# First-layer experts of a two-layer mixture-of-experts block: the gate and up product made from high and low halves

## What is computed

```python
w, idx = jax.lax.top_k(probs, TOP_K)                       # 8 of 64
gu_e = jnp.einsum('ech,ehf->ecf', buf, expert_gate_up_w)   # [rows of e, 512] x [512, 2 * 256]
act = _silu(gu_e[..., :I]) * gu_e[..., I:]
out_e = jnp.einsum('eci,eih->ech', act, expert_down_w)     # [rows of e, 256] x [256, 512]
y = out_e[e_flat, slot] * w_flat[:, None]                  # summed over a token's 8 experts
```

## Time and profile before

| what | value |
|---|---|
| median of 3 runs | 2224.71 us |
| the profiled execution: time / span | 2228.88 us / 2227.1 us |
| TensorE busy | 2103.2 us, 94% |
| VectorE / ScalarE / GpSimd busy | 59% / 47% / 23% |
| mean granted TensorE clock | 0.976 |
| first-layer experts, first to last tile's start | 695.55 to 1112.48 us |

### The profile page before, as it was taken

How to read it: one execution, slowest core, us unless ns; L and a number is a source line. 1 busy time by engine, 2 the same in 40 slices (tenths; PEclk the granted TensorE clock), 3 DMA queues, 4 the chain that set the end, 5 groups by cost and what they waited for, 6 DMA issues and landing times. The chain is left out here.

```text
span 2227.1 us, 39923 instructions
## 1 busy us (share of the span) xinstructions
PE 2103.2 (94%) x13454; PEld 1518.7 (68%) x13455; DVE 1310.5 (59%) x2799; ACT 1049.0 (47%) x2427; POOL 522.1 (23%) x503
## 2 busy tenths in 40 slices
PE   6999999998998999999978999999989989999998
PEld 3777777775964444444465777788759867777775
DVE  4677777776773222222255777777664437777776
ACT  2466666666321111111133666666665316666655
POOL 4000000001553545445512000000002302223332
PEclk9999999997999999999989999999979999999999
DMA  5001000103142989998831000000032156656661
GB/s 175 29 33 34 22 18 33 34 2 138 38 189 80 332 281 318 321 328 279 257 92 54 22 11 25 28 28 28 1 124 88 39 210 234 253 205 223 228 220 19
DMA packets 63471, 282.47 MB, mean 127 GB/s; under 512 B 13155, under 2 KB 13325, under 8 KB 44005
## 3 DMA queue, kind: packets, MB, share of 16 engines
q1 hardware_dynamic: 43604, 246.88, 30.0%
q0 software_dynamic: 19728, 33.75, 6.9%
HBM read 259.82 MB, written 32.41 MB: 131 GB/s over the span
## 5 line engine op out<-in xcount | busy, mean ns | idle before, releaser
L818 ACT ACTIVATE probs<-ps,less_max 100x360 f32<-100x360 f32 (+1 forms) x384 | 212.0, 561 | 167.5 <-DVE less_max L648 88.3
L1811 PE MATMUL pgu<-ring,xT 128*128 x560 | 267.0, 600 | 6.5 <-issue 3.3
L804 ACT ACTIVATE pTs<-pt 128x300 f32<-128x300 f32 x512 | 189.3, 425 | 128.7 <-PE pt L527 127.6
L1811 PEld LDWEIGHTS pgu<-ring,xT 128*128 128x128 f32 x560 | 99.6, 191 | 114.8 <-issue 114.4
L527 PE MATMUL pt<-ident,probs 100*128 100x100 f32 (+1 forms) x1152 | 137.2, 256 | 30.8 <-ACT pTs L804 27.3
L527 PEld LDWEIGHTS pt<-ident,probs 100*128 100x128 f32 (+1 forms) x1152 | 115.9, 141 | 61.4 <-issue 36.8
L404 PE MATMUL po<-first 128*128 128x512 f32 (+1 forms) x564 | 146.9, 411 | 1.4 <-DVEq L706 1.4
L1899 DVE COPY hT<-ph 128x256 f32<-128x256 f32 x70 | 29.7, 425 | 195.9 <-PE ph L1817 195.9
L404 PE MATMUL pp<-first 128*128 128x512 f32 x564 | 143.2, 402 | 1.2 <-DVE first L428 1.2
L648 DVE CUSTOM_DVE_ANT_0 ps<-ps,madd 100x362 f32<-100x362 f32 (+1 forms) x256 | 128.8, 566 | 23.7 <-PE ps L513 23.5
L400 PE MATMUL po<-first 128*128 128x362 f32 (+1 forms) x720 | 136.9, 339 | 2.8 <-DVE first L437 1.4
(11 more groups left out here) (352 smaller groups left out, 4457.3 us busy)
## 6 DMA issues: line engine op xcount, KB each, us to landing
ring<-in_l_ew SPq DMA_DIRECT2D x64, 1536.0 KB, 9.5
w<-in_l_ew SPq DMA_DIRECT2D x40, 1024.0 KB, 7.9
after<-in_l_ew SPq DMA_DIRECT2D x24, 1024.0 KB, 8.1
xnT<-in_ctxT SPq DMA_DIRECT2D x14, 1444.0 KB, 6.6
first<-in_l_up SPq DMA_DIRECT2D x2, 4096.0 KB, 13.4
b<-in_l_eb SPq DMA_DIRECT2D x8, 1024.0 KB, 4.7
wd<-in_l_down SPq DMA_DIRECT2D x2, 2048.0 KB, 8.7
xn_rows<-mid SPq DMA_DIRECT2D x16, 200.0 KB
```

Source lines behind the costliest of these rows:

```text
L804: act.activation(pTs[:, g % 2, j, 3 * half:3 * half + 3, :].rearrange("k c q -> k (c q)"), pt[:, half, 0:3 * S], ACT.Copy).then_inc(t_out, 1)
L818: act.activation(probs[g % 2 * HPC + j][:, k0:k1], ps[j][0:S, 0:k1 - k0], ACT.Exp, bias=less_max[:, g, seg, j:j + 1], scale=-1.0 if masked ...
L1811: last = pe.matmul(pgu[p][:, :], xT[p][:, c, :], wgu[c], start=c == 0, stop=c == DC - 1)
```

## The change

- `gate_up` in the first layer makes three float32r products a chunk, of high and low halves of rows and of weights, in place of one float32 product: 12 matmuls a tile for four.
- ScalarE gains for each tile a copy of the turned rows (`xT_high`) and a copy of the weights of the tile after the next, 128 x 2048, to `ws_high`. Its order is silu, rows, weights, `y`.
- VectorE's copy of the rows becomes a subtraction out of PSUM (`xT_low`), and it gains a subtraction of the next tile's weights, 128 x 2048 with both inputs in SBUF (`ws_low`), placed between `hT` and `xT_low`.
- TensorE no longer reads the expert's number nor the place for `gate_up`. ScalarE and VectorE read the place. GpSimd reads the expert's number of the tile three ahead, after that tile's gather, waits for `w_ready` there and passes it on as `weights_there`.
- SyncE passes on `w_ready` for three places ahead of the one it replaces, not two. Two small loads for the next stage wait for `parts_done`, as they share memory with the halves.
- The two tables get two more entries, which repeat the last tile.

The diff, with three hunks left out (the first table's two entries, the small loads' wait, the sizes of the tables):

```diff
@@ -1567,6 +1569,7 @@
                         link(dve.scalar_tensor_tensor(out=texp[:, :], in0=turn_of[:, :], scalar=-float(RING),
                                                       in1=texp[:, :], op0=ALU.mult, op1=ALU.add))
                         link(dve.tensor_copy(env.tile_buffer[:, 0:NT], texp[:, :]))
+                        link(dve.tensor_copy(env.tile_buffer[:, NT:NT + 2], texp[:, NT - 1:NT].broadcast_to([1, 2])))
 
                     step = 2 if swiglu else 1
                     evens = tile_n[:, :].rearrange("a (n s) -> a n s", s=step)[:, :, 0]
...
@@ -1657,11 +1660,15 @@
         index_now = [sb(f"index_now{p}", [P, 1], U32) for p in range(2)]
         sum_at = [sb(f"sum_at{p}", [P, 1], U32) for p in range(2)]
         xg = [sb(f"xg{p}", [P, D]) for p in range(2)]
-        xT = [sb(f"xT{p}", [P, DC, P]) for p in range(2)]
+        xT = [sb(f"xT{part}", [P, DC, P], F32R) for part in ("_high", "_low")]
         sg = [sb(f"sg{p}", [P, I0]) for p in range(2)]
         h = [sb(f"h{p}", [P, I0]) for p in range(2)]
         hT = [sb(f"hT{p}", [P, FI, P]) for p in range(2)]
         y = [sb(f"y{p}", [P, D]) for p in range(2)]
+
+        ws = [[sb(f"ws{p}{part}", [P, DC, 2 * I0], F32R) for part in ("_high", "_low")] for p in range(2)]
+        weights_there = sem("weights_there")
+        x_high, gu_high, gu_low, parts_done = sem("x_high"), sem("gu_high"), sem("gu_low"), sem("parts_done")
         px, ph = pb("px", [P, DC, P]), pb("ph", [P, 4, P])
         pgu = [pb(f"pgu{p}", [P, 2 * I0]) for p in range(2)]
         pd = [pb(f"pd{p}", [P, D]) for p in range(2)]
...
@@ -1682,6 +1689,11 @@
         def pairs_of(engine):
             return engine.value_load(env.tile_count[0:1, 0:1], min_val=MIN_PAIRS0, max_val=TILES0 // 2)
 
+        def gate_up_weights(engine, t):
+            at = slice(t, t + 1) if isinstance(t, int) else bass.ds(t, 1)
+            place = engine.value_load(env.tile_buffer[0:1, at], min_val=0, max_val=RING - 1)
+            return ring[:, bass.ds(place, 1), 0:DC, :].rearrange("p a c n -> p (a c) n")
+
         with nc.Block() as block:
             @block.sync
             def _(sp):
...
@@ -1695,14 +1707,14 @@
 
                 def replace(turn, n):
 
-                    ahead = n + 2
+                    ahead = n + 3
                     arrived(ahead % RING, turn - 1 + ahead // RING)
                     e = turn * RING + (n - RING)
                     at = slice(e, e + 1) if isinstance(e, int) else bass.ds(e, 1)
                     ended = sp.value_load(env.tile_ends[0:1, at], min_val=1, max_val=TILES0)
                     sp.wait_ge(d_mm, ended)
                     load(turn * RING + n, n)
-                for n in range(2):
+                for n in range(3):
                     arrived(n, 0)
                 turns, rest = E0 // RING, E0 % RING
                 with sp.Fori(1, turns) as turn:
...
@@ -1761,18 +1775,30 @@
                         out=env.moe_sum[p][:, :], in_=y[p][:, :], in_offset=None, compute_op=ALU.add,
                         out_offset=bass.IndirectOffsetOnAxis(ap=sum_at[p][:, 0:1], axis=0),
                         bounds_check=T - 1, oob_is_err=False).then_inc(added[p], 16)
+                def tiles_weights(t):
+
+                    at = slice(t, t + 1) if isinstance(t, int) else bass.ds(t, 1)
+                    e = pool.value_load(env.tile_expert[0:1, at], min_val=0, max_val=E0 - 1)
+                    pool.wait_ge(w_ready, e + 1)
+                    pool.sem_inc(weights_there, 1)
+                for p in range(2):
+                    tiles_weights(p)
                 for p in range(2):
                     fetch(2 + p, p)
+                for p in range(2):
+                    tiles_weights(2 + p)
                 pool.wait_ge(env.sum_begun, 16 * G)
                 pool.sem_inc(passed, 1)
                 pool.wait_ge(env.x_out, 16 * B)
                 pool.sem_inc(passed, 1)
                 for p in range(2):
                     fetch_next(2, p)
+                    tiles_weights(4 + p)
                     add_rows(0, p, True)
                 with pool.Fori(3, n_pairs + 1) as i:
                     for p in range(2):
                         fetch_next(i, p)
+                        tiles_weights(i * 2 + p)
                         add_rows(i - 2, p)
                 last = last_pair_of(pool)
                 for p in range(2):
...
@@ -1793,22 +1819,21 @@
                         last = pe.transpose(px[:, c, :], rows[p][:, c * P:(c + 1) * P], ident[:, :])
                     last.then_inc(x_mm, 1)
 
-                def weights(t, row):
+                def down_weights(t):
                     at = slice(t, t + 1) if isinstance(t, int) else bass.ds(t, 1)
                     place = pe.value_load(env.tile_buffer[0:1, at], min_val=0, max_val=RING - 1)
-                    return [ring[:, bass.ds(place, 1), row + n, :].rearrange("p a n -> p (a n)")
-                            for n in range(DC if row == 0 else FI)]
+                    return [ring[:, bass.ds(place, 1), DC + n, :].rearrange("p a n -> p (a n)") for n in range(FI)]
 
                 def gate_up(t, p, between):
-                    at = slice(t, t + 1) if isinstance(t, int) else bass.ds(t, 1)
-                    e = pe.value_load(env.tile_expert[0:1, at], min_val=0, max_val=E0 - 1)
-                    wgu = weights(t, 0)
-                    pe.wait_ge(w_ready, e + 1)
+                    pe.wait_ge(gu_low, t + 1)
                     pe.wait_ge(x_ready, t + 1)
                     for c in range(DC):
                         if c == DC // 2:
                             between()
-                        last = pe.matmul(pgu[p][:, :], xT[p][:, c, :], wgu[c], start=c == 0, stop=c == DC - 1)
+                        for i, j in PARTS:
+                            last = pe.matmul(pgu[p][:, :], xT[i][:, c, :], ws[p][j][:, c, :],
+                                             start=c == 0 and (i, j) == PARTS[0],
+                                             stop=c == DC - 1 and (i, j) == PARTS[-1])
                     last.then_inc(gu_mm, 1)
 
                 def hidden_turned(t, p):
...
@@ -1859,17 +1884,34 @@
                 def silu(t, p):
                     act.wait_ge(gu_mm, t + 1)
                     act.activation(sg[p][:, :], pgu[p][:, 0:I0], ACT.Silu).then_inc(silu_done, 1)
-                silu(0, 0)
-                silu(1, 1)
+                def x_high_out(t):
+                    act.wait_ge(x_mm, t + 1)
+                    act.activation(xT[0][:, :, :], px[:, :, :], ACT.Copy).then_inc(x_high, 1)
+
+                def split_high(t, p, wgu):
+                    act.wait_ge(weights_there, t + 1)
+                    act.activation(ws[p][0][:, :, :], wgu, ACT.Copy).then_inc(gu_high, 1)
+
+                def units(t, p):
+
+                    wgu = gate_up_weights(act, t + 2)
+                    silu(t, p)
+                    x_high_out(t + 1)
+                    split_high(t + 2, p, wgu)
+                x_high_out(0)
+                for p in range(2):
+                    split_high(p, p, gate_up_weights(act, p))
+                units(0, 0)
+                units(1, 1)
                 row_out(0, 0, 0, True)
-                silu(2, 0)
+                units(2, 0)
                 row_out(1, 0, 1, True)
-                silu(3, 1)
+                units(3, 1)
                 row_out(2, 1, 0)
                 with act.Fori(2, n_pairs) as i:
-                    silu(i * 2, 0)
+                    units(i * 2, 0)
                     row_out(i * 2 - 1, i - 1, 1)
-                    silu(i * 2 + 1, 1)
+                    units(i * 2 + 1, 1)
                     row_out(i * 2, i, 0)
                 act.wait_ge(raw_in[0], 16)
                 for k0, k1 in SPLIT:
...
@@ -1878,6 +1920,8 @@
                 last_pair = last_pair_of(act)
                 row_out(last_pair * 2 + 1, last_pair, 1)
 
+                act.wait_ge(gu_low, last_pair * 2 + 3)
+                act.sem_inc(parts_done, 1)
                 for n in range(2):
                     act.wait_ge(raw_in[n + 1], 16)
                     act.activation(env.wide_first[2 * n][:, :, :], env.raw_ahead[n][:, :, :], ACT.Copy).then_inc(w_high, 1)
...
@@ -1886,9 +1930,15 @@
             def _(dve):
                 n_pairs = pairs_of(dve)
 
-                def rows_out(t, p):
-                    dve.wait_ge(x_mm, t + 1)
-                    dve.tensor_copy(xT[p][:, :, :], px[:, :, :]).then_inc(x_ready, 1)
+                def rows_out(t):
+                    dve.wait_ge(x_high, t + 1)
+                    dve.tensor_tensor(xT[1][:, :, :], px[:, :, :], xT[0][:, :, :].bitcast(F32), ALU.subtract)\
+                        .then_inc(x_ready, 1)
+
+                def split_low(t, p, wgu):
+                    dve.wait_ge(gu_high, t + 1)
+                    dve.tensor_tensor(ws[p][1][:, :, :], wgu, ws[p][0][:, :, :].bitcast(F32), ALU.subtract)\
+                        .then_inc(gu_low, 1)
 
```

(8 more changed lines are left out.)

11 lines of the change are left out of this document (7 added, 4 removed).

## The result

The changed kernel takes 2276.36 us, the median of 4 runs (2271.96 to 2284.38), against 2225.10 us (2222.96 to 2228.01, 4 runs) for the kernel before. The ratio is 1.0234, with a 95% interval of 1.0213 to 1.0255. That is outside the forecast range. It went the way of rival 2, and further.

What follows compares the result with a forecast made beforehand. TensorE and DMA were taken as close bounds, with VectorE's 5.31 us the new shortest period and 5.6 us expected for 37 tiles. -7.8 + 4.5 + 0.5 = -2.8 us gave a median of 2222 us, range 2202 to 2250.

Steps and rivals of the forecast that it cites:

- rival 2: First-layer experts: GpSimd becomes the bound, a read held by `ws_low` every tile, 6.19 us a tile; 2244 to 2252 us; chance 0.30.
- The products: TensorE, gate and up: twelve float32r products take 2.74 us in place of 3.44; TensorE alone 5.11 us a tile.
- VectorE's circle: VectorE's `hT`, `ws_low`, `xT_low` up to TensorE's next start: shortest period 5.31 us.
- GpSimd's reads: GpSimd instructions can't begin during VectorE's subtraction of two SBUF inputs; the adding DMA taken as held, up to 2.29 us.
- A period of 5.51 us lets it in: GpSimd's adding misses the next `ws_low` by 0.2 us at 5.31 us a tile; 5.51 us lets it start.
- 37 tiles: Of the stage's 69 periods, those of 5.81 to 5.85 us without a TensorE gap; forecast at 5.6 us, -7.8 us together.
- the 32 others: Remaining periods of the 69, where TensorE or ScalarE waits for rows the DMA carries; bound by landings, left at 6.3 us.
- The DMA: Loads unchanged, 5.58 us of transfers a tile: 5.6 us for 37 periods, 6.3 for the rest.
- rival 1: The queues give way: 37 tiles at 5.31 us, 2211 us, or 2195 if the rest gain half a microsecond; chance 0.25.
- The start: First tile: `xT_high`, `ws_high` and `ws_low` in line before TensorE, 5.1 us in place of 1.0; taken as +4.5 us.
- The end: ScalarE makes an unused weight copy before the last but one `y`: +0.5 us, bounds 0 and 0.8.
- rival 3: Weights come too late: GpSimd waits before `sum_at` for weights three tiles ahead; +40 us, 2264 us; chance 0.05.

Runs made afterwards that it cites:

- four pieces: The changed kernel with VectorE's subtraction of the weights (`ws_low`) cut into four pieces of 128x512, the work otherwise the same: 2225.59 us, ratio 0.9996 to the kernel before.

## Why the prediction was wrong

- **The products: right.** TensorE alone was put at 5.11 us a tile; without the subtraction its shortest period is 5.17.
- **VectorE's circle: right.** 5.31 us forecast, 5.24 the shortest seen. By itself it costs little: the subtraction with one SBUF input adds 5 us to the run without any.
- **GpSimd's reads: right that the adding is held too** (3.25 us for 1.59). The Trainium skill (SBUF — State Buffer, "Who interferes with whom") infers the contrary for the making of descriptors; the gather's 2.46 us and the adding's 3.25 us speak against it here. The same section says that a VectorE instruction with at most one SBUF input, outside its two-port modes, doesn't contend with GpSimd. The run with one SBUF input agrees, with 1.07 and 1.59 us. `index_now` was put near 0.7 us in the mean and came to 1.08; the forecast saw only holds, and most of these copies stand behind an adding instead.
- **The step that failed** is "A period of 5.51 us lets it in". With 5.6 us for the new period the forecast took the adding to be let in, and gave the hold no price at all. Both halves of that are wrong. The undisturbed periods are 5.24 to 5.26 us, not 5.6, so by the forecast's own sum the adding has no room. And a missed adding doesn't lengthen TensorE's period: the forecast took GpSimd and TensorE as one rigid circle, in which a delay on one side moves the other. TensorE's only large wait for GpSimd is the one for gathered rows (45.4 us; behind the first tile its matmuls wait at most 1.6 us in sum for the work of any other engine), and rows gathered ahead put it off. TensorE keeps its 5.25 us while GpSimd needs more, so `ws_low` moves on against GpSimd's chain from tile to tile, and each of its instructions comes into the hold in turn: all 71 subtractions hold one. What was put at nothing measured 2276.4 - 2219.1 = 57 us. The argument against rival 2, that a delay of 0.2 us in TensorE's start lets the adding in, falls with it. That this depends on TensorE's pace is shown by the run with more products: slower by work, the kernel is 19 us faster.
- **Rival 2 had the mechanism and its floor** (6.19 us a tile; 6.29 to 6.34 between addings with half the loads). Its size was too small, 2244 to 2252 us, since it lengthened 37 tiles and left the 32 others almost alone. With GpSimd as the bound all 69 are on it. In the changed kernel the 37 periods that were undisturbed before last 6.64 us in the mean, the 32 others 6.48. With half the loads the mean over all is 6.33, with the full loads 6.57, where a gather takes 6.6 us to land and not 4.8 (medians). What part of the 0.24 us is landing, and what part the lower clock after each wait, I haven't separated.
- **The DMA: right in the sum by luck.** The forecast had 5.6 us for the 37 undisturbed periods and left the 32 others at 6.3, a mean of 5.92. In the run without the subtraction the mean is 5.85, but the same 37 last 5.78 us and the same 32 last 5.92, not 6.3 (5.76 and 5.97 with one SBUF input). So the 37 gained next to nothing on 5.81 us, and the 32, which were said to be bound by landings that the change does nothing for, gained 0.4 us each. With half the loads as well they are 5.30 and 5.25 us: the amount of transfers sets both. The two errors nearly cancel. That is why, without the hold, the sum was near: 2222 us forecast, 2219.1 with one SBUF input, 2225.6 in four pieces.
- **Two ends of ranges are slips.** The forecast's own range begins at 2213 us, which leaves out the 4.1 us of the start (2224.7 - 11.1 + 4.1 = 2217.7). A third of rival 1's further 16 us gives 2206, not 2202. Neither bears on the outcome.
- **The start: right.** +4.6 us for 4.5. The lower clock came on top: the first tile's products are 0.43 us apart (699.27, 699.70), not 0.23, and the first period is 7.6 us, 6.7 before. The forecast gave 0.4 us to that.
- **The end: +3.1 us for 0.5.** The last but one `y` comes 1157.88 - 1155.55 = 2.3 us after the turned rows, as forecast (2.4). But `y` of the last tile waits 2.21 us for an adding DMA, and the last adding goes out 13.6 us after the last tile's start, 11.2 before. That is the hold again: with one SBUF input the end takes 22.3 us, with four pieces 22.4, against 22.65 before.
- **Rivals 1 and 3.** Once nothing is held, the share goes to 1 and the 69 periods gain 13.6 us, between the forecast's 7.8 and rival 1's 18.5. But the gain lies in the 32 disturbed periods, which rival 1 had as its second part, and not in the 37. The weights were in time; taking the wait off GpSimd changed 3 us, within the noise.
